# Delta-rule layer: chain in blocks of 8 steps, batch by batch, and a W/U stage with separate PSUM banks

## The reference, cut to what matters

```python
def step(Sst, inp):
    q_t, k_t, v_t, b_t, g_t = inp
    Sst = Sst * g_t[..., None, None]
    kS = jnp.einsum('bhk,bhkv->bhv', k_t, Sst)
    Sst = Sst + b_t[..., None, None] * jnp.einsum('bhk,bhv->bhkv', k_t, v_t - kS)
    o_t = jnp.einsum('bhk,bhkv->bhv', q_t, Sst)
    return (Sst, o_t)
_, out = jax.lax.scan(step, S0, (qt, kt, vt, bt, gt))
```

## Time and profile before

| what | us |
|---|---|
| median of 3 runs (5107.34 to 5110.77) | 5109.11 |
| the profiled execution, its own time | 5108.61 |
| its span | 5106.9 |
| stretch of `phase_mix` (3397 to 3638) | 241.0 |
| from there to the first product of the chain (3638 to 3658) | 20.0 |
| stretch of the chain (3658 to 4093.3) | 435.3 |

### The profile page before, as it was taken

One profiled execution on the slowest core, in us unless ns is written; L12 is line 12 of the kernel. 1 busy time (PEld: TensorE's weight loads), 2 busy tenths in 40 slices (PEclk: granted clock), 3 DMA queues, 4 the chain that ended last, 5 costly groups with the idle time before them and its releaser, 6 DMA issues. The chain is left out here.

```text
span 5106.9 us, 109157 instructions
## 1 busy us (share of the span) xinstructions
PE 3737.7 (73%) x37201; PEld 1984.0 (39%) x37203; DVE 2733.6 (54%) x5646; ACT 2108.3 (41%) x3466; POOL 1172.7 (23%) x2077
## 2 busy tenths in 40 slices
PE   6699999999999995528585447026444469789999
PEld 3233333333333332416363226016333346444478
DVE  5688888888888884812123654751133434423433
ACT  0177777777777774214242213013222212243322
POOL 4321121121122110162003730724200013311100
PEclk8799999999999997769797765557555579889999
DMA  1400000000000002044533323334433110040053
GB/s 44 168 35 0 0 0 0 0 0 0 0 0 0 0 0 78 25 156 152 173 119 103 116 84 122 90 106 161 86 42 46 23 56 4 11 157 25 4 186 131
DMA packets 256377, 319.78 MB, mean 63 GB/s; under 512 B 27729, under 2 KB 177489, under 8 KB 256209
## 3 DMA queue, kind: packets, MB, share of 16 engines
q1 hardware_dynamic: 243920, 283.86, 19.0%
q0 software_dynamic: 12288, 33.57, 2.0%
HBM read 181.58 MB, written 135.79 MB: 62 GB/s over the span
## 5 line engine op out<-in xcount | busy, mean ns | idle before, releaser
L791 DVE TENSOR_REDUCE att_maxes<-att_ps_m 128x1 f32<-128x512 f32 x2048 | 1342.0, 689 | 337.2 <-PE att_ps_m L648 324.0
L755 ACT ACTIVATE att_prob<-att_ps_s 128x1024 f32<-128x1024 f32 x1024 | 992.7, 1021 | 439.5 <-PE att_ps_s L658 429.5
L648 PE MATMUL att_ps_m<-att_k_t,att_q_t 96*128 96x512 bf16 x2048 | 792.8, 387 | 22.4 <-DVE att_maxes L791 4.8
L658 PE MATMUL att_ps_s<-att_q_t,att_k_t 99*128 99x512 bf16 x2048 | 612.6, 380 | 1.8 <-ACT att_q_t L741 1.7
L670 PE MATMUL att_ps_o<-att_prob,att_v_h 128*32 128x512 f32 x4096 | 546.3, 605 | 0.8 <-DVE att_o_sum L804 0.5
L648 PEld LDWEIGHTS att_ps_m<-att_k_t,att_q_t 96*128 96x128 bf16 x2048 | 196.6, 96 | 696.9 <-DVE att_maxes L791 595.0
L562 POOL CAST att_max_parts<-att_neg_max 128x4 bf16<-128x4 f32 x128 | 24.7, 193 | 1306.6 <-DVE att_neg_max L798 1306.6
L1359 DVE TENSOR_TENSOR experts_h<-experts_gs,experts_ps_g 128x128 f32<-128x128 f32 x192 | 55.4, 288 | 468.3 <-ACT experts_gs L1340 466.4
L658 PEld LDWEIGHTS att_ps_s<-att_q_t,att_k_t 99*128 99x128 bf16 x2048 | 190.7, 98 | 206.4 <-issue 31.7
L2209 ACT ACTIVATE chain_faded<-chain_state,chain_gam 128x32 f32<-128x32 f32 x512 | 126.6, 311 | 330.0 <-DVE chain_state L2233 320.6
L1312 PE MATMUL experts_ps_g<-w_gu,experts_x_t 128*128 x768 | 217.9, 406 | 35.6 <-ACT experts_x_t L1336 18.9
(11 more groups left out here) (346 smaller groups left out, 6398.5 us busy)
## 6 DMA issues: line engine op xcount, KB each, us to landing
slots_x<-zeros SPq DMA_DIRECT2D x97, 256.0 KB, 3.3
experts_xs<-slots_x SPq DMA_DIRECT2D x48, 512.0 KB
slots_y<-experts_y SPq DMA_DIRECT2D x48, 512.0 KB
logits_t<-sstat_logit SPq DMA_DIRECT2D x64, 256.0 KB
xf_t<-logits_t SPq DMA_DIRECT2D x8, 2048.0 KB
proj<-comb_pr SPq DMA_DIRECT2D x8, 1600.0 KB
mix_pr<-proj SPq DMA_DIRECT2D x32, 400.0 KB
w_d<-in_L_ffn_wd SPq DMA_DIRECT2D x2, 4096.0 KB, 20.0
```

Of the source, the lines that this page charges most:

```text
L648: pe.matmul(ps_m[i % 2][:, :], q_t[0:PAIRS, p, tile * P:(tile + 1) * P], k_t[0:PAIRS, p, c * W:(c + 1) * W], start=True, stop=True).then_i ...
L658: mm = pe.matmul(ps_s[half][:, i * W:(i + 1) * W], k_t[0:ROWS, p, tile * P:(tile + 1) * P], q_t[0:ROWS, p, chunk * W:(chunk + 1) * W], sta ...
L755: nc.scalar.activation(prob[:, i % RING, :, :].rearrange("q a w -> q (a w)"), ps_s[half][:, :], ACT.Exp, scale=SCALE).then_inc(expd.sem, 1)
L791: v.tensor_reduce(maxes[:, p, tile, c:c + 1], ps_m[i % 2][:, :], X, ALU.max).then_inc(reduced.sem, 1)
```

## The change

In `phase_chain` CB goes from 16 to 8, and PE and DVE go through the whole step of batch 0 before that of batch 1. The loop body then holds 2 blocks of 8 = 16 steps and runs 8 times. In `phase_mix` the results of `first`, `second` and the transposes go to PSUM tensors of one bank each, two of each kind (`ps_x`, `ps_y`, `ps_t`); the transposes become a third stage, two tiles behind `first`; the loads, outputs and `nat` have four buffers instead of two, and with them the unrolling goes from 2 tiles to 4; the widening of the factors is cut into one half for T and one for P; POOL's scaling is cut into two stages. The decay at the chunks' ends (`gam_col`), before made in each tile, is loaded once by one DMA of small rows, spread by POOL, turned by four transposes ahead of the first tile and copied out by one ACT instruction at the end.

```diff
-        ps = [ph.ps(f"ps{i}", [P, HG, GP]) for i in range(2)]
+        ps_x = [ph.ps(f"ps_x{i}", [P, GP]) for i in range(2)]
+        ps_y = [ph.ps(f"ps_y{i}", [P, GP]) for i in range(2)]
+        ps_t = [ph.ps(f"ps_t{i}", [P, GP]) for i in range(2)]
+        ps_e = ph.ps("ps_e", [P, GP])
...
+                sp.dma_start(ends[:, :, :], factors.rearrange("(i n t) a h -> n i t a h", i=B, t=CL)[:, :, CL - 1, 0, :]).then_inc(ends_in, 16)
...
-            staged(sp, NT, load, idle, store)
+            staged(sp, NT, load, idle, idle, store, unroll=LOADS)
...
-            staged(pool, NT, scale)
+            staged(pool, NT, scale_kv, scale_qk, unroll=LOADS)
...
             def first(t, p):
-                pe.wait_ge(widened.sem, widened.at(t))
-                pe.wait_ge(scaled.sem, scaled.at(t, 3))
-                pe.wait_ge(w_q_kept.sem, w_q_kept.before(t))
+                pe.wait_ge(wide_t.sem, wide_t.at(t))
+                pe.wait_ge(kv_scaled.sem, kv_scaled.at(t))
+                pe.wait_ge(x_kept.sem, x_kept.before(t))
...
-                for half in range(KD):
-                    mm = pe.matmul(ps[p][:, 1, half * CPT:(half + 1) * CPT], gam_k[:, p, half * 8:(half + 1) * 8, :].rearrange("q h d -> q (h d)"),
-                                   ident[:, CL - 1:P:CL], start=True, stop=True, skip_group_check=True)
...
-            staged(pe, NT, first, second)
+            staged(pe, NT, first, second, turn, unroll=LOADS)
...
-            staged(act, NT, widen, keep_x, keep_w_q)
+            staged(act, NT, widen_t, idle, keep_x, idle, keep_w_q, unroll=LOADS)
...
-            staged(v, NT, keep_y)
+            staged(v, NT, keep_y, unroll=LOADS)
...
-CB = 16
+CB = 8
...
                         mm.then_inc(w_s[b].sem, 1)
-                    for b in range(B):
                         pe.wait_ge(us[b].sem, us[b].at(t, c + 1))
...
                                         ps_w[own, :, 0:32], ALU.subtract).then_inc(us[b].sem, 1)
-                    for b in range(B):
-                        sets = slice(KD * b, KD * b + KD)
                         v.wait_ge(k_us[b].sem, k_us[b].at(t, c + 1))
```

More of the change, by code:

```diff
@@ L77, in before @@
     def before(self, t, p):
-        return t * (16 * self.per) + (32 - 16 * p) * self.per
+        step = 32 // self.ring
+        return t * (step * self.per) + (32 - step * p) * self.per
 def hold(eng, gate):
@@ L161, in steps, with transfers @@
         return Steps(self.sem(name), per, ahead)
[L163 to L164 removed]
+    def transfers(self, name, per=1, soft=False, ring=2):
+        return Transfers([self.sem(f"{name}{p}", soft) for p in range(ring)], per, soft)
     def block(self):
@@ L1935, in _ @@
                 s.prime(sp)
+            with nc.allow_non_contiguous_dma("the decay at each chunk's end"):
+                sp.dma_start(ends[:, :, :], factors.rearrange("(i n t) a h -> n i t a h", i=B, t=CL)[:, :, CL - 1, 0, :]).then_inc(ends_in, 16)
             def load(t, p):
-                sp.wait_ge(scaled.sem, scaled.before(t))
+                sp.wait_ge(kv_scaled.sem, kv_scaled.before(t))
                 hold(sp, gate)
-                sp.wait_ge(widened.sem, widened.before(t))
+                sp.wait_ge(qk_scaled.sem, qk_scaled.before(t))
+                hold(sp, gate)
+                sp.wait_ge(wide_t.sem, wide_t.before(t))
+                hold(sp, gate)
+                sp.wait_ge(wide_p.sem, wide_p.before(t))
                 hold(sp, gate)
@@ L1992, in _ @@
                 s.prime(pe)
+            pe.wait_ge(ends_wid, 1)
+            for i in range(B):
+                for half in range(KD):
+                    c = (i * KD + half) * P
+                    mm = pe.transpose(ps_e[:, c:c + P], ends_wide[:, i, half * HALF:(half + 1) * HALF, :].rearrange("q h d -> q (h d)"), ident[:, :])
+            mm.then_inc(ends_turned, 1)
             def first(t, p):
-                pe.wait_ge(widened.sem, widened.at(t))
-                pe.wait_ge(scaled.sem, scaled.at(t, 3))
-                pe.wait_ge(w_q_kept.sem, w_q_kept.before(t))
+                pe.wait_ge(wide_t.sem, wide_t.at(t))
+                pe.wait_ge(kv_scaled.sem, kv_scaled.at(t))
+                pe.wait_ge(x_kept.sem, x_kept.before(t))
                 hold(pe, gate)
[L1999 to L2005, removed]
+                for h in range(H):
+                    for r in range(4):
+                        own = slice(32 * r, 32 * r + 32)
+                        mm = pe.matmul(ps_x[p % 2][own, 32 * h:32 * h + 32], wide[own, p % 2, place(h), :, :].rearrange("q a t -> q (a t)"),
+                                       k_v[own, p % 2, h, :, :].rearrange("q a d -> q (a d)"), start=True, stop=True, skip_group_check=True)
                 mm.then_inc(firsts.sem, 1)
@@ L2009, in second, with turn @@
                 pe.wait_ge(x_kept.sem, x_kept.at(t))
+                pe.wait_ge(wide_p.sem, wide_p.at(t))
+                pe.wait_ge(y_kept.sem, y_kept.before(t))
                 hold(pe, gate)
[L2011 to L2016, removed]
-                                           nat[own, p, 0:2, h, :], start=True, stop=True, skip_group_check=True)
+                for h in range(H):
+                    for r in range(4):
+                        own = slice(32 * r, 32 * r + 32)
+                        mm = pe.matmul(ps_y[p % 2][own, 32 * h:32 * h + 32], wide[own, p % 2, H + place(h), :, :].rearrange("q a t -> q (a t)"),
+                                       nat[own, p, 0:2, h, :], start=True, stop=True, skip_group_check=True)
                 mm.then_inc(seconds.sem, 1)
+            def turn(t, p):
                 pe.wait_ge(y_kept.sem, y_kept.at(t))
-                pe.wait_ge(scaled.sem, scaled.at(t, 5))
+                pe.wait_ge(w_q_kept.sem, w_q_kept.before(t))
                 for half in range(KD):
```

108 lines of the change are left out of this document (61 added, 47 removed).

## The result

| | before | after |
|---|---|---|
| median, us | 5108.34 (5107.34 to 5110.77, 4 runs) | 5181.46 (5178.95 to 5184.90, 4 runs) |
| span of the profiled execution | 5106.9 | 5183.2 |
| W/U stage, from SP's first DMA to the chain's clearing | 240.7 | 306.3 |
| from there to the chain's first product | 19.6 | 10.6 |
| chain, first to last product | 435.2 | 457.3 |

The kernel became slower: 5181.46 / 5108.34 = 1.0143, with a 95% interval of 1.0128 to 1.0158. That is +73 us, where +131 was forecast. The two parts went differently: the W/U stage got worse by 65.6 us (forecast 52), the chain with its start by 22.1 - 9.0 = 13.1 us (forecast 79). Among the experiments one execution each of cb8_inter (6788.90 us) and cb16_serial (17812.56 us) fell in a slower state; only fast executions are compared.

What follows compares the result with a forecast made beforehand. The prediction took PE's latency loop and instruction fetch to bound the chain, and PE's products and waits the W/U stage. Its sum was 5109 + 79 (chain) + 52 (W/U stage) = 5240 us, range 5060 to 5310.

Steps and rivals of the forecast that it cites:

- The loops' sizes: PE's new loop bodies, some 2048 records in the chain and 2080 in the W/U stage, are both too long to stay.
- The chain's order: Chain: batch by batch, u1 collides with batch 0's states at DVE; a step takes 2.72 us against 1.99, +93 us.
- part of the stalls under DVE's waits: Chain: in a slower step part of a fetch lies under a wait for DVE, for a third of 67 stalls; -12 us.
- four more returns: Chain: 7 returns of the loop instead of 3, each 4.65 us where a block costs 2.2; +10 us.
- loads' hold-ups: Chain: a block's loads hold up a fetch (8.80 us); with twice as many of half the length, -5 us.
- The W/U stage: W/U stage: bound by fetching 67 blocks at 3.88 us, plus returns, fill, setup and held-up fetches; 293 against 241 us, +52.
- the forecast's own case: Whole kernel: both loops miss PE's store and the chain's order costs; 5180 to 5310 us, chance 0.52.
- The rival of fixed places: PE's store: 8 blocks, each with a fixed place, only blocks sharing one are lost; 5083 us, chance 0.2.
- The rival of a store that holds both loops: PE's store: the chain's and W/U stage's loops both stay, fetched only once; 4970 us, chance 0.18.
- The chain's fetches: Chain: as many instructions, so 180 us of fetch stay; +10 for returns, -5 for loads, -12 for stalls under waits.
- The third rival: Chain: both loops miss, but the fetch runs beside the slower step; chain about -5, in all 5155 us, chance 0.1.
- Without fetches PE would be the bound at 4.4 us a tile: W/U stage: unfetched, its three stages overlap; products 1.7 + 1.74, transposes 0.65, semaphores 0.3 make 4.4 us a tile.

Runs made afterwards that it cites:

- cb8_inter: The kernel before with only CB cut from 16 to 8, batches interleaved as before; 5053.49 us, ratio 0.9889.
- cb16_serial: The kernel before with only the new batch-by-batch order, blocks still 16 steps; ratio 1.0107 (5244.89 us where the kernel before took 5185.89).
- light kernels: cb16_light and cb8_light: the kernel before with only the first step of each block loaded, blocks of 16 or 8; ratios 0.9917 and 0.9894.
- cb16_light: The kernel before, all DMAs kept but only the first of a block's 16 steps loaded; ratio 0.9917 (5143.62 us where the kernel before took 5185.89).
- mix_only: The kernel after with the chain of the kernel before (blocks of 16, batches interleaved); 5175.13 us, ratio 1.0131.
- cb8_light: cb16_light with CB = 8, so blocks of 8 steps with only the first loaded; ratio 0.9894 (5130.45 us where the kernel before took 5185.89).
- chain_only: The kernel before with both chain edits (blocks of 8, batch by batch), W/U stage of before; 5125.57 us, ratio 1.0033.
- mix_short: mix_only with PE's W/U loop cut from four tiles to two (1060 instructions) and two `nat` buffers; 5069.65 us, ratio 0.9917.
- mix_lead: mix_short with SP's stores moved one turn later; ratio 0.9828 (5094.41 us where the kernel before took 5185.89).
- cb4_inter: The kernel before with CB cut from 16 to 4, batches interleaved as before; 4940.57 us, ratio 0.9671.
- cb4_serial: The kernel before with CB = 4 and the batch-by-batch order of the kernel after; 5007.61 us, ratio 0.9837.

## Why the prediction was right and wrong

| step of the prediction | forecast | measured |
|---|---|---|
| The loops' sizes | both are fetched in each pass | 63 packets in the W/U loop, 70 in the chain |
| The chain's order, a step | 2.72 us, +93 | 2.61 us, +79 |
| part of the stalls under DVE's waits | -12 | -9 (469.1 - 334 = 135, 9 below 399.0 - 255 = 144) |
| four more returns | +10 | 0 within 0.1 (light kernels) |
| loads' hold-ups | -5 | -36 in the chain with blocks of 8 (cb8_inter); all the bytes are worth 34 (cb16_light) |
| The chain's start | -7 | -9.0 |
| The W/U stage | +52 | +65.6, mix_only 71 |

The total lies at the lower edge of the forecast's own case (5180 to 5310). It got there by two errors of unlike size and sign: the W/U stage was 14 us worse than forecast, the chain 66 us better. The sign was reasoned out; that the sum came so near was in part luck.

**The loops' sizes** is the step that decided the sign, and it held. No run has a body between 1526 instructions of all kinds (attention's loop) and 2116, so the border lies between them. The rival of fixed places is out: with it the W/U loop would have had four or five packets in each pass, and it has ten. The rival of a store that holds both loops is out by the 63 and 70 packets.

**The chain's order** held in its mechanism, row by row, and nearly in its size: u of batch 1 starts behind the states of batch 0 and a step is 0.62 us longer.

**The chain's fetches** is the step that failed. The sentence was "there are twice as many of half the length, which I take as -5". It had 8.80 us of one such fetch in its own row, 6.6 above a plain block of 2.2. PE's timeline of the kernel before has seven stalls of the kind: 33 us were there to be counted. The estimate took it for granted that half a burst does about half the harm, twice as often. cb16_light shows that the loads' bytes are worth 34 us in all, and cb8_light against cb8_inter that with half a burst nothing is left of it. The four returns at +10 bring no packet of their own (71 either way), and the 180 us to which they were added already held every packet; why the longer stalls at them cost nothing in sum is open. With -34 and 0 in place of -5 and +10 the chain's sum is 93 - 34 - 12 - 7 = 40; with the measured 79 for the order it is 26, and chain_only's stretches give 25. The kernel after has 13, since its chain is 12 shorter than the same chain there, for a reason that stays open.

The third rival (the fetch runs beside the slower step, chain -5, in all 5155) was closer to the chain's number and to the total than the forecast, but not by its mechanism. With the order alone 60 to 72 us of the 79 remain at every size of block, so the fetch is not hidden by the slower step.

**The W/U stage** held: bound by fetches. By the forecast's terms a pass of four tiles is 8.5 blocks at 3.88 and a return at 2.4, with its share of the 8 us for held-up fetches 36.2 us. It takes 38.2 on average (six passes from 3447.00 to 3676.25), so 2.0 were missing in each of seven passes: 14 us, as much as the stage was missed by.

"Without fetches PE would be the bound at 4.4 us a tile" was wrong for the stage as the change writes it. mix_short's loop takes 11.5 us for two tiles, 5.75 each, since the loads are late. With the loads in time mix_lead takes 7.9 for two, so 3.95 each, near the number, but not by its mechanism. The sum of 4.4 had products of 1.7 us a set; at the clock of 1.00 the sets take 1.28, and PE has 1.28 + 1.28 + 0.65 = 3.2 us of work a tile. The rest is mostly a wait for ACT, and ACT waits for the loads, with the DMA engines 84% busy. PE is not the bound there. That the number is near is luck. The prediction costed the edits on other engines at nothing and looked at busy time only; it didn't ask what SP's load stands behind, nor what the transfers of a tile take. Under the fetches of the kernel after this hides. It shows as soon as they go.

Two slips in the working moved nothing: the chain has 8192 + 8180 = 16372 records in the earlier trace rows, not 16700, and with each of the 67 blocks held up 1 us more the upper bound of the stage is +119, not +105.

## What to carry to other kernels

Count the instructions of an engine's loop body before unrolling it further: here a body of 1060 instead of 2116 was worth 108 us, and one of 1078 instead of 2148 (cb4_inter against cb8_inter) 113, while 2148 instead of 4294 was worth nothing by itself. The waits saved in the W/U stage, 2.3 us a tile, were worth less than the fetches that came with the longer body. Where a fetched loop shares the DMA engines with bursts of loads, read the longest "issue" stall at the loads and multiply it by their number; and when a bound is removed, look at the order of the DMA-issuing queue next.

## What the runs showed of the hardware

- Bodies of 1060, 1078 and (attention) 1526 instructions stay: no packet, or a single one, in all their later passes. Those of 2116, 2148 and 4294 are fetched whole in every pass (10, 9 and 17 to 18 packets). In the fetched chains a stall comes every 256 instructions, counting matmuls, weight loads, waits and register instructions.
- A block costs a PE that runs small matmuls 1.8 to 2.5 us of the chain on average; a loop's return 3.7 to 5.5 where the body is fetched (4.06 in the kernel after) and 0.5 where it is resident (cb4_serial), against 0.1 at a change of block without a return.
- Loads of data hold up an instruction packet: 8.80 us behind a whole block's loads, 1.95 with the same DMAs and a sixteenth of their bytes.
- The granted clock was lower where PE stood for fetches or loads: 0.50 in the kernel after's W/U stage, 0.73 in mix_short's and 1.00 in the middle of mix_lead's. In the chain it is 0.50 in all kernels, and there shorter stalls bring no faster products.
- The phases ahead of the W/U stage, with unchanged code, took 3386 to 3399 us on the first two chips and 3464 to 3474 on the third. The W/U stage of the kernel before could still be compared: 239.7 to 242.0 us in the first sets, 240.6 to 242.0 in the last.
